# A six-stage decoder kernel on one core: the gated-linear-attention loop in another order, its value and gate products in three f16 passes, and the scales of the last weights moved

## The chip, the core and the metric

The kernel runs on one NeuronCore of a Trainium2 chip. Its engines have queues of their own and meet only through semaphores: TensorE (PE; its weight loads are shown as PEld), VectorE (DVE), ScalarE (ACT), GpSimd (POOL) and SyncE (SP), which here only issues DMAs. The metric is the device time of one execution in microseconds, lower is better; a kernel's time is the median of its runs.

## The reference, cut to what matters

The reference is a decoder of two layers over 2 x 512 tokens of width 128, with six residual stages: gated linear attention (GLA), cross attention to 77 context rows, a layer with a small attention and eight experts, an attention with 16 heads and a position bias, a bidirectional attention with the context, and a feed-forward layer with quantised weights. The change lies in the first stage and in the preparation for the last:

```python
def step(S, inp):
    qt, kt, vt, gt = inp
    S = jnp.exp(gt)[:, None] * S + kt[:, None] * vt[None, :]
    return (S, qt @ S)
...
v = (x @ Wv).reshape(b, t, H, HV).transpose(0, 2, 1, 3)
o = jax.vmap(jax.vmap(_gla_scan))(q, k, v, g)
o = o * jax.lax.rsqrt(jnp.mean(o * o, axis=-1, keepdims=True) + EPS) * rms_w
o = o.reshape(b, t, DV) * jax.nn.silu(x @ Wg)
```

and, for the last stage, `scale = 127.0 / amax` per column of `W_in` and per row of `W_out`, with the weights rounded on that scale.

## The kernel before, in words

Tokens stand in eight tiles of 128 (`NT`), four to each of the two sequences (`TG`). The kernel is one program in which each engine's instructions are written out in order, with explicit semaphores (`sm[...]`): an engine waits with `wait_ge` and everything behind the wait in its queue waits too. No planner sets the order.

The GLA scan is done in chunks of 64 tokens (`CH`), two to a tile. Around the loop of lines 1115 to 1127 TensorE does five things for a tile `i`, each a function:

- `gla_kv(i)` (line 1059): the keys of each chunk times its values, two matmuls of 256 columns on the two 64-row halves of the array (64*128). DVE's `gla_state` turns them into the running state `ST`.
- `gla_a(i)` (L1042): keys times queries, two matmuls of 256 columns on the two 64-column halves (128*64). DVE's `gla_mask` writes the masked product to `AM`.
- the first half of `gla_o(i)` (L1070): `AM` times the values, four matmuls of 64 columns, each with weights of its own, on the whole array (128*128).
- the second half of `gla_o(i)` (L1077): the queries times the state, on 64-column halves again. Its end (`o_mm`) lets ACT square the sum (`take_o`, L704), after which DVE multiplies it with the gate (`gate_out`, L1746), which frees the bank (`ob_ready`).
- `gla_vg(i + 2)` (L1084): the values and the gate of the tile two ahead, one f32 matmul of 512 columns on the whole array. ACT copies the values out (L687) and applies the SiLU (L690).

An f32 matmul shows as two instructions in the trace. The order in an iteration is kv(i), a(i+1), o(i) in its two halves, vg(i+2), so the shape of the array tile changes five times. On DVE the order of an iteration `i` is `gla_state(i)`, `gla_mask(i + 1)`, `gate_out(i - 1)`, and in iterations 1 to 3 one part of `weight_scales` (L1769 to L1779), which takes the maxima of the last stage's weights `wC` and the scales from them; its last part raises `ws_ready`. In iteration 6 `head_norm(0)` (L1754) follows, and TensorE's `gla_t(0)`, in iteration 7, waits for it.

The waits that matter in the loop are these:

```python
# gla_o(i), ahead of its first half
pe.wait_ge(sm["kpt_ready"], min(i, 1) + 1)
pe.wait_ge(sm["am_ready"], i + 1)
if i >= 2:
    pe.wait_ge(sm["ob_ready"], i - 1)
```

that is, the masked product of tile i and `gate_out(i - 2)`. In iteration 0, `keys_t(1)` (four transposes, after DVE's `keys_out(1)`, L1696) stands behind `gla_o(0)`.

POOL sets constants, scales the output weights in `wA` (L415), waits for DVE's queries (`qs_ready`), spreads them over `QX` (L424, L430) and expands the keys of the context (L437). Later, during the cross attention, it splits the first experts' weights (L479, L481), then waits for `ws_ready` and rounds the last weights in four instructions (`quantise_weights`, L461 to L468), then copies the attention values of the first sequence (L494, `at_pool`), for which TensorE's `attended_t(0)` waits. DVE's queue at the end of the cross attention is: `norm_stats(2, 0, X)`, `ctx_norm(6)`, `norm_rows(3, 0, X, Z)`, `norm_rows(2, 0, X, Y)`, `ctx_norm(7)`, the residual; some way on come the products of queries and keys `PR` (L1864).

`norm_rows` is line 1648, `take_yt` (the copy of the transposed normed rows to `YT`, semaphore `ln_yt`) line 640, `keep_busy` (matmuls of ones whose result nobody reads) line 972, and every transpose line 967.

Of the kernel before, what the change touches and what calls it, by code (L numbers as in the profile page):

```python
# [4 lines left out]


# [1 line left out]

# [1 line left out]

# [4 lines left out]
F16 = mybir.dt.float16  # L15
# [5 lines left out]
NT = 8  # L21
# [86 lines left out]
def build(nc, x, cols, rows, wa, gk2, wb, wc, ctx_rows, cst, spread, of_head, onehot, rel_bias, w1, w2, twqkv, two, out):  # L108
    bias_dram = nc.dram_tensor("bias_rows", [TH, P, NREL], F32, kind="Internal").ap()
    stack = ExitStack()  # L110
    with stack:
# [78 lines left out]
        with ExitStack() as held:  # L190
            def gla(name, shape):
                return held.enter_context(nc.sbuf_tensor(name, shape, F32))

            H1 = gla("H1", [LR, TOK])
            U = gla("U", [P, TOK])
            LA = gla("LA", [P, TOK])
            reset = gla("reset", [P, TOK])
            G = gla("G", [P, TOK])
            GC = gla("GC", [P, TOK])
            dG = gla("dG", [P, NC])  # L200
            E0 = gla("E0", [P, TOK])
# [12 lines left out]
            KVM = gla("KVM", [P, DV])  # L214
            ST = gla("ST", [P, 4, DV])
            OB = gla("OB", [P, NT, DV])
            SQ = QX[:, 0:NT // 2, :, :].rearrange("p t h c -> p (t h c)").rearrange("p (t d) -> p t d", d=DV)
            SS = gla("SS", [P, NT * GH])
            SL = gla("SL", [P, NT * GH])
            SR = gla("SR", [P, NT * GH])  # L220
            OT = V[:, :, :].rearrange("p t d -> p (t d)").rearrange("p (n c) -> p n c", n=2)
# [38 lines left out]
        with ExitStack() as held:  # L260
# [53 lines left out]

        names = """ld_x ld_cs ld_a ld_b ld_c ld_d bias_dma dve_c act_c qx_ready qx_pool konst_ready
            ln_var ln_rstd ln_y ln_tp ln_yt x_done
            qk_mm gk_mm h1_ready rc_ready u_ready l_ready g_ready e_ready kp_ready qs_ready kp_tp kpt_ready vg_mm vg_ready
            a_mm am_ready kv_mm st_ready o_mm ob_ready sq_ready sr_ready og_ready ot_mm ot_ready go_mm
            cx_mm cx_copied cx_parts vx_ready vs_mm vb_ready qt_mm qt_hi qt_ready xb_ready s_mm px_sub px_ready pt_mm pt_ready xo_mm ct_ready ws_ready co_mm
            qkv_mm qkv_ready sc_ready se_ready at_pool at_ready att_mm att_ready pr_mm h2_ready rt_mm lg_ready le_ready xh_ready  # L320
            ym_hi ym_ready w1_split w2_split w1_ld0 w1_ld1 w2_ld0 w2_ld1 hid_mm gel_ready hid_hi hid_lo eo_mm acc_ready
            bias_mm bias_ready tw0 tw1 tw_split ld_wo ld_band strip_ready ow_ready ctw_ready
            pj_mm pj_hi pj_ready ts_mm ttr_ready ttr_turn exp_ready rps_ready rpp_ready raw_ready tt_mm pta_ready ptb_ready tpv_mm ctt_ready wo_mm to_ready
            rh_ready rj_mm rj_ready bs_mm m_ready as_sub as_exp as_ready ast_mm ast_ready hq_mm ast_low hq_ready mt_mm mrow_ready mb_mm nm_ready eb_ready hb_mm w0_ready f_mm
            wq_ready wqt_mm win_ready ax_ready ax_mm am_one ab_mm nr_ready yr_ready zs_ready zr_ready zt_mm zt_ready hm_mm ht_ready hq2_ready fo_mm st_out""".split()
        sm = {n: sem(n) for n in names}
# [69 lines left out]
        def _(pool):  # L396
# [566 lines left out]
        def _(pe):  # L963
# [24 lines left out]
            def wA_(name, n):  # L988
                return wA[:, WA[name]:WA[name] + n]
# [69 lines left out]
                    mm(bank[2 + r][:, 0:DV], KPT[CH * r:CH * r + CH, i, :], V[CH * r:CH * r + CH, i, :],  # L1059
                       start=True, stop=True).then_inc(sm["kv_mm"], 1)  # L1060

            def gla_o(i):
                pe.wait_ge(sm["kpt_ready"], min(i, 1) + 1)
                pe.wait_ge(sm["am_ready"], i + 1)
                if i >= 2:
                    pe.wait_ge(sm["ob_ready"], i - 1)
                o = bank[4 + i % 2]
                firsts = 2 * i % CB == 0
                for h in range(GH):
                    ins = mm(o[:, GV * h:GV * h + GV], AM[:, i % 2, h, :], V[:, i, GV * h:GV * h + GV],  # L1070
                             start=(h == 0), stop=False, skip_group_check=True)
                for r in range(2):
                    c = 2 * i + r
                    if c % CB == 0:
                        continue
                    pe.wait_ge(sm["st_ready"], c // CB * (CB - 1) + c % CB)
                    ins = mm(o[CH * r:CH * r + CH, 0:DV], QP[:, CH * c:CH * c + CH], ST[:, c % 4, :],  # L1077
                             start=False, stop=True, skip_group_check=True)
                ins.then_inc(sm["o_mm"], 1)

            def gla_vg(t):

                pe.wait_ge(sm["vg_ready"], gate_at(t - 2))
                mm(bank[6 + t % 2][:, :], YT[:, P * t:P * t + P], wA_("vg", 2 * DV), start=True, stop=True).then_inc(sm["vg_mm"], 1)  # L1084

            def gla_t(g):

# [26 lines left out]
            keep_busy(5, 2)  # L1114
            for i in range(NT):
                gla_kv(i)
                if i + 1 < NT:
                    gla_a(i + 1)
                if i == NT - 1:
                    gla_t(0)  # L1120
                    spread_values()
                    gla_out(0)
                gla_o(i)
                if i == 0:
                    keys_t(1)
                if i + 2 < NT:
                    gla_vg(i + 2)

            def queries(g):

# [494 lines left out]
        def _(dve):  # L1625
# [157 lines left out]
            for i in range(NT):  # L1783
                gla_state(i)
                if i + 1 < NT:
                    gla_mask(i + 1)
                if i >= 1:
                    gate_out(i - 1)
                if 1 <= i < TG:
                    weight_scales(i - 1)  # L1790
                if i == NT - 2:
                    head_norm(0)
            gla_residual(0)
# [36 lines left out]
            for i in range(NT):  # L1830
                if i == NT - 1:

                    dve.wait_ge(sm["x_done"], 3)
                    norm_stats(2, 0, X)
                if i == TG + 1:
                    dve.wait_ge(sm["co_mm"], TG)
                    dve.wait_ge(sm["xb_ready"], 1)
                    residual(0, XB, 7, 1)
                if i == NT - 1:
                    ctx_norm(NT - 2)  # L1840
                if i + 1 < NT:
                    subtract_max(i + 1)
                if i == 0:
                    norm_rows(1, 1, X, Y)
                if i == 1:
                    query_low(1)
# [137 lines left out]
            def t5_step(i, n, s, last):  # L1984
# [9 lines left out]
                if on(s, 1, last):  # L1994
                    if r1 % ROWS == 0:
                        dve.wait_ge(sm["strip_ready"], (i * 2 + r1 // ROWS + 1) * 6)
                    if s >= 5:
                        dve.wait_ge(sm["tt_mm"], (n - 4) * 2)
                    dve.wait_ge(sm["ts_mm"], n * 2)
                    dve.sem_inc(sm["ttr_turn"], 1)  # L2000
# [353 lines left out]
```

## Time and profile before

| | us |
|---|---|
| median of 3 runs | 471.5 |
| the runs | 470.9, 471.5, 475.05 |
| span of the profiled execution, first to last instruction | 473.3 |
| TensorE busy in it | 437.0 (92%) |
| VectorE busy | 361.5 (76%) |
| ScalarE busy | 287.7 (61%) |
| GpSimd busy | 212.3 (45%) |

The profiled execution has no other time of its own beside its span; the span lies between the runs and 1.8 above their median. In the rows of the timeline the columns are: start in us from the span's start, length in us, engine, line, operation, what is written and read, shapes, how many instructions the row merges, and in brackets the idle time of that engine just before, with what released it. Matmul lengths overlap each other, so the distance from start to start is what a stage takes.

### The profile page before, as it was taken

To read this page: it belongs to the slowest core of one execution; us is meant where nothing else is said; L and a number is where in the kernel's file an instruction comes from. 1 tells how busy PE (TensorE), PEld (TensorE's weight loads), DVE (VectorE), ACT (ScalarE), POOL (GpSimd) and SP (SyncE) were. 2 spreads that over 40 slices of the span, in tenths; PEclk is the share of its full clock that TensorE was granted. 3 is DMA by queue.
4 is the path that set the end of the run, shared out by engine and by line. 5 is a ranking of instruction groups with operands and counts; after the bars stand their busy time and mean duration, and the time that the engine had idled before them with its cause. 6 is when DMAs were issued, how large, how long until landed. Compare 5 with 4: busy or idle time off the path is not lost.

```text
span 473.3 us, 13124 instructions
## 1 busy us (share of the span) xinstructions
PE 437.0 (92%) x4544; PEld 311.4 (66%) x4544; DVE 361.5 (76%) x984; ACT 287.7 (61%) x684; POOL 212.3 (45%) x548
## 2 busy tenths in 40 slices
PE   8999887997789998699999999999999997998887
PEld 6555565776667777367666666666666665887756
DVE  3897659775779989777778787777787867557786
ACT  3753436874368874577777777777777776423450
POOL 5160011650123557037766668576666676440200
PEclk9999799998989999899999999999999999999989
DMA  7499936400001131000000000000000000000001
GB/s 218 76 98 100 98 39 201 156 4 1 0 2 35 44 91 35 1 1 18 3 18 3 1 17 14 3 0 0 0 0 0 2 1 2 1 3 1 1 0 46
DMA packets 15622, 15.81 MB, mean 33 GB/s; under 512 B 1348, under 2 KB 12859, under 8 KB 15579
## 3 DMA queue, kind: packets, MB, share of 16 engines
q1 hardware_dynamic: 15579, 15.24, 15.9%
q8 instruction: 26, 0.43, 0.4%
q14 instruction: 17, 0.14, 0.1%
HBM read 10.52 MB, written 4.72 MB: 32 GB/s over the span
## 4 chain that ended last, share of the span: by engine, by line
PE 74%; DVE 18%; ACT 4%; issue 3%; DMA 1%; POOL 0%; SPq 0%; DVEq 0%; ACTq 0%; POOLq 0%
PE bank L967 16%; PE bank L1484 12%; PE bank L1436 10%; PE bank L1359 5%; PE bank L1280 3%; PE bank L1267 3%; PE bank L1477 3%; PE bank L1355 3%; PE bank L1168 2%; PE bank L1374 2%; DVE Y L1648 1%; PE bank L972 1%; PE bank L1070 1%; PE bank L1084 1%; PE bank L1618 1%
## 5 line engine op out<-in xcount | busy, mean ns | idle before, releaser
L877 ACT ACTIVATE SN<-SN,nmx 128x512 f32<-128x512 f32 x128 | 92.7, 725 | 9.7 <-DVE nmx L2016 7.6
L967 PE MATMUL bank<-cs,SN 128*128 128x128 f32 x512 | 67.7, 275 | 3.3 <-DVE Z L2009 1.6
L967 PEld LDWEIGHTS bank<-cs,SN 128*128 128x128 f32 x512 | 57.7, 142 | 18.4 <-issue 12.5
L1436 PE MATMUL bank<-TK,TQ 64*128 64x512 f16 x384 | 52.6, 380 | 1.4 <-DVE TK L1979 1.4
L552 POOL TENSOR_TENSOR CTW<-YT 128x128 f32<-128x128 f32 x64 | 29.6, 462 | 50.9 <-DVE YT L2014 50.6
L2001 DVE CUSTOM_DVE_ANT_0 SN<-bank,strip 128x512 f32<-128x512 f32 x64 | 43.3, 677 | 1.2 <-PE bank L1436 0.6
L2016 DVE CUSTOM_DVE_ANT_0 SN<-bank,strip 128x512 f32<-128x512 f32 x64 | 43.6, 681 | 0.0
L2009 DVE COPY PTO<-bank 128x512 f32<-128x512 f32 x32 | 22.1, 691 | 21.0 <-PE bank L1484 19.2
L972 PE MATMUL bank<-ones 128*128 128x128 f32 x230 | 34.8, 310 | 1.0 <-POOL konst L400 1.0
L972 PEld LDWEIGHTS bank<-ones 128*128 128x128 f32 x230 | 32.5, 222 | 3.9 <-issue 2.5
L2009 DVE COPY Z<-bank 128x512 f32<-128x512 f32 x32 | 22.1, 691 | 16.8 <-PE bank L1484 14.3
L888 ACT COPY PTO<-bank 128x512 f32<-128x512 f32 x32 | 18.7, 586 | 26.1 <-PE bank L1484 26.1
L1484 PE MATMUL bank<-PTO,TV 128*64 128x128 f32 x512 | 33.4, 273 | 0.0
L1484 PE MATMUL bank<-Z,TV 128*64 128x128 f32 x512 | 33.4, 273 | 0.0
L888 ACT COPY Z<-bank 128x512 f32<-128x512 f32 x32 | 18.7, 585 | 22.5 <-PE bank L1484 22.3
L556 POOL TENSOR_TENSOR CTX<-CTW,CTX 128x128 f32 (+1 forms) x64 | 27.4, 428 | 10.0 <-POOL CTX L554 8.7
L554 POOL TENSOR_TENSOR CTX<-CTW,ones 128x128 f32 (+1 forms) x64 | 25.7, 401 | 10.5 <-POOL CTW L552 9.3
L1359 PE MATMUL bank<-YP,WP 128*128 128x512 f16 x96 | 27.2, 398 | 0.6 <-DVE YP L1968 0.6
L2014 DVE COPY YT<-bank 128x256 f32<-128x256 f32 x64 | 26.6, 415 | 1.3 <-PE bank L1484 1.3
L1484 PEld LDWEIGHTS bank<-Z,TV 128*64 128x64 f32 x512 | 27.3, 137 | 0.0
L1484 PEld LDWEIGHTS bank<-PTO,TV 128*64 128x64 f32 x512 | 27.3, 137 | 0.0
L1908 DVE TENSOR_TENSOR HID<-PT,HID 128x512 f16<-128x512 f32 x32 | 24.8, 816 | 2.6 <-ACT HID L809 2.3
(326 smaller groups left out, 965.6 us busy)
## 6 DMA issues: line engine op xcount, KB each, us to landing
bias_rows<-biasr SPq DMA_DIRECT2D x1, 4096.0 KB, 45.2
band<-bias_rows SPq DMA_DIRECT2D x1, 3072.0 KB, 11.2
wqkv<-in_twqkv SPq DMA_DIRECT2D x8, 192.0 KB, 2.7
w1s<-in_w SPq DMA_DIRECT2D x8, 128.0 KB, 2.1
w2s<-in_w SPq DMA_DIRECT2D x8, 128.0 KB, 2.1
wB<-in_wb SPq DMA_DIRECT2D x1, 753.0 KB, 6.0
wA<-in_wa SPq DMA_DIRECT2D x1, 520.0 KB, 4.7
X<-in_x SPq DMA_DIRECT2D x2, 256.0 KB, 3.3
```

Of the source, the lines that this page charges most:

```text
L552: gp.tensor_tensor(CTW[:, :], raw[:, 0:P], raw[:, P:2 * P], ALU.mult).then_inc(sm["ctw_ready"], 1)
L556: gp.tensor_tensor(dst[:, 1, :], CTW[:, :], dst[:, 0, :], ALU.subtract).then_inc(sm["ctt_ready"], 1)
L877: sc.activation(p, p, ACT.Exp, bias=nmx[:, r % RING, h:h + 1], scale=-1.0, accum_out=psm[:, r % RING, h:h + 1]).then_inc(sm["exp_ready"], 1)
L888: sc.copy(probs_t(r, 0), bank[4][:, :]).then_inc(sm["pta_ready"], 1)
L967: return nc.tensor.transpose(out_, in_, ident[0:n, 0:n])
L972: mm(bank[b][:, 2 * P:3 * P], ones[:, :], ones[:, :], start=True, stop=True)
L1359: ins = mm(o[:, :], WP[u][:, w_part, w:w + P], YP[:, x_part, S * g:S * g + S], start=(k == 0), stop=(k == 2))
L1436: ins = mm(bank[2 * (s % 2) + h][:, :], TQ[u][r, q_part, S * b + P * qt:S * b + P * qt + P], TK[u][r, k_part, S * b:S * b + S], start=(k = ...
L1484: ins = mm(bank[6][d, 0:P], TV[u][:, TG * b + kt, d], probs_t(r, h)[:, P * kt:P * kt + P], start=(kt == 0), stop=(kt == TG - 1))
L2001: vv.tensor_tensor_reduce(out=SN[:, r1 % RING, 0, :], in0=bank[2 * (r1 % 2)][:, :], in1=strip[u1][:, 0, c1:c1 + S], scale=-1.0, scalar=3.0 ...
L2009: vv.tensor_copy(probs_t(r, 1), bank[5][:, :]).then_inc(sm["ptb_ready"], 1)
L2016: vv.tensor_tensor_reduce(out=SN[:, r1 % RING, 1, :], in0=bank[2 * (r1 % 2) + 1][:, :], in1=strip[u1][:, 1, c1:c1 + S], scale=-1.0, scalar ...
```

## The change

1. The loop's order on TensorE becomes kv(i), first half of o(i) (now `gla_inside`), vg(i+2), a(i+1), second half of o(i) (now `gla_before`). In iteration 0 `keys_t(1)` stands behind `gla_inside(0)`; in iteration 7 `gla_t(0)`, `spread_values` and `gla_out(0)` stand ahead of `gla_inside(7)` as they stood ahead of `gla_o(7)`. The waits of the halves are the same. DVE's and ACT's orders in the loop stay, but for 3.
2. `gla_vg` of tiles 2 to 7 multiplies f16 halves in three passes (high x high, high x low, low x high). POOL makes them before it scales `wA`: two instructions on the 512 columns of the weights, two on the 256 of tiles 2 and 3, two on the 512 of tiles 4 to 7. Tiles 0 and 1 stay f32.
3. The three parts of `weight_scales` leave the loop and stand in the cross attention's last iteration, behind `ctx_norm(6)` and ahead of `norm_rows(3, 0, X, Z)`.
4. The increments of a semaphore that nobody waits for (`ttr_turn`) go to the new semaphore `vg_split`.

```diff
+            def split_gla(dst, w, n):
+                gp.tensor_tensor(dst[:, 0, :], w, ones[:, 0:1].to_broadcast([P, n]), ALU.mult).then_inc(sm["vg_split"], 1)
+                at = next(parts)
+                pool.wait_ge(sm["vg_split"], at)
+                gp.tensor_tensor(dst[:, 1, :], w, dst[:, 0, :], ALU.subtract).then_inc(sm["vg_split"], 1)
+
+            parts = itertools.count(1, 2)
+            pool.wait_ge(sm["ld_a"], 48)
+            split_gla(WVG, wA[:, WA["vg"]:WA["vg"] + 2 * DV], 2 * DV)
+            for g, (a, b) in enumerate(((2 * P, S), (S, TOK))):
+                pool.wait_ge(sm["ln_yt"], g + 1)
+                split_gla(YG[:, :, a - 2 * P:b - 2 * P], YT[:, a:b], b - a)
...
                 pe.wait_ge(sm["vg_ready"], gate_at(t - 2))
-                mm(bank[6 + t % 2][:, :], YT[:, P * t:P * t + P], wA_("vg", 2 * DV), start=True, stop=True).then_inc(sm["vg_mm"], 1)
+                pe.wait_ge(sm["vg_split"], 4 if t < TG else 6)
+                for k, (x_part, w_part) in enumerate(PRODUCTS):
+                    ins = mm(bank[6 + t % 2][:, :], YG[:, x_part, P * (t - 2):P * (t - 1)], WVG[:, w_part, :], start=(k == 0), stop=(k == 2))
+                ins.then_inc(sm["vg_mm"], 1)
...
             for i in range(NT):
                 gla_kv(i)
-                if i + 1 < NT:
-                    gla_a(i + 1)
                 if i == NT - 1:
                     gla_t(0)
                     spread_values()
                     gla_out(0)
-                gla_o(i)
+                gla_inside(i)
                 if i == 0:
                     keys_t(1)
                 if i + 2 < NT:
                     gla_vg(i + 2)
+                if i + 1 < NT:
+                    gla_a(i + 1)
+                gla_before(i)
...
                 if i >= 1:
                     gate_out(i - 1)
-                if 1 <= i < TG:
-                    weight_scales(i - 1)
...
                 if i == NT - 1:
                     ctx_norm(NT - 2)
+                    for part in range(3):
+                        weight_scales(part)
```

## Rows read from the trace of the kernel before

**Rows 1.** The page: the chain that ended last, shares by engine.

```profile
PE 74%; DVE 18%; ACT 4%; issue 3%; DMA 1%; POOL 0%; SPq 0%; DVEq 0%; ACTq 0%; POOLq 0%
```

**Rows 2.** Windows: stretch, length, busy time of each engine, granted clock, DMA.

```profile
26.00:53.00 27.00, 27.00 (x152) 14.01 (x152) 22.76 (x52) 12.97 (x68) 5.96 (x11) 1.00 0.91 99
...
54.50:55.00 0.50, 0.15 (x1) 0.15 (x2) 0.50 (x2) 0.00 (x0) 0.00 (x0) 0.50 0.91 98
...
61.50:62.00 0.50, 0.50 (x7) 0.50 (x6) 0.00 (x0) 0.00 (x0) 0.00 (x0) 1.00 0.91 98
```

**Rows 3.** Timeline of TensorE, matmuls of one iteration of the GLA loop.

```profile
38.01 0.70 PE L1059 MATMUL bank<-V,KPT 64*128 64x256 f32 x2
38.63 0.65 PE L1042 MATMUL bank<-QX,KC 128*64 128x256 f32 x4
39.22 1.10 PE L1070 MATMUL bank<-V,AM 128*128 128x64 f32 x8
40.25 0.65 PE L1077 MATMUL bank<-ST,QP 128*64 128x256 f32 x4
40.83 1.12 PE L1084 MATMUL bank<-wA,YT 128*128 128x512 f32 x2
```

**Rows 4.** Timeline of TensorE's weight loads, the next iteration's first.

```profile
41.89 0.30 PEld L1059 LDWEIGHTS bank<-V,KPT 64*128 64x128 f32 x4 [0.76 <-issue]
```

**Rows 5.** Timeline of VectorE, one iteration without a part of the scales.

```profile
46.50 0.42 DVE L1737 TENSOR_TENSOR KVM<-bank,cs 128x256 f32<-128x256 f32 x1 [1.13 <-PE bank L1059]
...
48.46 0.86 DVE L1719 TENSOR_TENSOR AM<-bank,cs 64x256 f32<-64x256 f32 x2
...
49.35 0.42 DVE L1746 TENSOR_TENSOR OB<-bank,SG 128x256 f32<-128x256 f32 x1
...
50.39 0.42 DVE L1737 TENSOR_TENSOR KVM<-bank,cs 128x256 f32<-128x256 f32 x1 [0.62 <-PE bank L1059]
```

**Rows 6.** Timeline of TensorE, f16 passes of 512 columns in the experts.

```profile
141.95 2.12 PE L1267 MATMUL bank<-YM,w1p 128*128 128x512 f16 x9 [0.59 <-ACT PT L814]
```

**Rows 7.** Timeline of VectorE, keys of the second sequence, and the end of the loop.

```profile
26.60 1.10 DVE L1696 TENSOR_TENSOR KP<-KC,ED 128x512 f32<-128x512 f32 x1
...
53.58 1.22 DVE L1754 TENSOR_TENSOR OB<-OB,SR 128x1024 f32<-128x1024 f32 x1
```

**Rows 8.** Timeline of TensorE, eight transposes behind the loop and eight later.

```profile
54.85 1.97 PE L967 MATMUL bank<-cs,OB 128*128 128x128 f32 x8 [1.67 <-DVE OB L1754]
...
69.26 1.09 PE L967 MATMUL bank<-cs,OB 128*128 128x128 f32 x8 [0.59 <-DVE OB L1754]
```

**Rows 9.** Timeline of POOL and VectorE, start of the kernel and first iterations.

```profile
11.98 0.61 POOL L415 TENSOR_TENSOR wA<-wA,rmsc 128x256 f32<-128x256 f32 x1 [5.30 <-DMA rmsc<-in_rows]
...
15.79 0.69 DVE L1685 SCALAR_TENSOR_TENSOR U<-U,LA 128x512 f32<-128x512 f32 x1 [0.75 <-ACT LA L660]
...
28.11 1.22 POOL L437 TENSOR_TENSOR KX<-KB,inside 128x616 f16<-128x616 f32 x1
...
28.64 0.97 DVE L1738 SCALAR_TENSOR_TENSOR ST<-ST,E,KVM 128x256 f32<-128x256 f32 x1
...
35.46 0.48 DVE L1738 SCALAR_TENSOR_TENSOR ST<-ST,E,KVM 128x256 f32<-128x256 f32 x1
```

**Rows 10.** Timeline of VectorE, the scales in the loop, and the cross attention's end.

```profile
34.29 0.68 DVE L1773 TENSOR_REDUCE amw<-wC 128x4 f32<-128x512 f32 x1
...
41.31 0.20 DVE L1777 RECIPROCAL scw<-amw 128x8 f32<-128x8 f32 x1
...
111.04 1.12 DVE L1648 TENSOR_SCALAR Y<-X,mv,rstd 128x128 f32<-128x128 f32 x4 [2.92 <-ACT rstd L633]
...
119.72 1.70 DVE L1864 TENSOR_TENSOR PR<-QKV 128x128 f32<-128x128 f32 x8 [1.65 <-ACT QKV L775]
```

**Rows 11.** Timeline of POOL, rounding of the last weights, attention values.

```profile
91.51 1.90 POOL L461 TENSOR_TENSOR WQ<-wC,scw 128x1024 f32<-128x1024 f32 x1
...
116.42 1.03 POOL L494 COPY AT<-QKV 128x128 f32<-128x128 f32 x4 [15.30 <-ACT QKV L775]
```

More of the change, by code:

```diff
@@ L7 @@
 from contextlib import ExitStack
+import itertools
 import numpy as np
@@ L217, in build @@
             SQ = QX[:, 0:NT // 2, :, :].rearrange("p t h c -> p (t h c)").rearrange("p (t d) -> p t d", d=DV)
+            YG = held.enter_context(nc.sbuf_tensor("YG", [P, 2, TOK - 2 * P], F16))
+            WVG = held.enter_context(nc.sbuf_tensor("WVG", [P, 2, 2 * DV], F16))
             SS = gla("SS", [P, NT * GH])
@@ L316, in build @@
             ln_var ln_rstd ln_y ln_tp ln_yt x_done
-            qk_mm gk_mm h1_ready rc_ready u_ready l_ready g_ready e_ready kp_ready qs_ready kp_tp kpt_ready vg_mm vg_ready
+            qk_mm gk_mm h1_ready rc_ready u_ready l_ready g_ready e_ready kp_ready qs_ready kp_tp kpt_ready vg_mm vg_split vg_ready
             a_mm am_ready kv_mm st_ready o_mm ob_ready sq_ready sr_ready og_ready ot_mm ot_ready go_mm
@@ L322, in build @@
             bias_mm bias_ready tw0 tw1 tw_split ld_wo ld_band strip_ready ow_ready ctw_ready
-            pj_mm pj_hi pj_ready ts_mm ttr_ready ttr_turn exp_ready rps_ready rpp_ready raw_ready tt_mm pta_ready ptb_ready tpv_mm ctt_ready wo_mm to_ready
+            pj_mm pj_hi pj_ready ts_mm ttr_ready exp_ready rps_ready rpp_ready raw_ready tt_mm pta_ready ptb_ready tpv_mm ctt_ready wo_mm to_ready
             rh_ready rj_mm rj_ready bs_mm m_ready as_sub as_exp as_ready ast_mm ast_ready hq_mm ast_low hq_ready mt_mm mrow_ready mb_mm nm_ready eb_ready hb_mm w0_ready f_mm
@@ L1060, in gla_kv, with gla_inside @@
                        start=True, stop=True).then_inc(sm["kv_mm"], 1)
-            def gla_o(i):
+            def gla_inside(i):
                 pe.wait_ge(sm["kpt_ready"], min(i, 1) + 1)
@@ L1066, in gla_o, with gla_before @@
                     pe.wait_ge(sm["ob_ready"], i - 1)
-                o = bank[4 + i % 2]
-                firsts = 2 * i % CB == 0
                 for h in range(GH):
-                    ins = mm(o[:, GV * h:GV * h + GV], AM[:, i % 2, h, :], V[:, i, GV * h:GV * h + GV],
-                             start=(h == 0), stop=False, skip_group_check=True)
+                    mm(bank[4 + i % 2][:, GV * h:GV * h + GV], AM[:, i % 2, h, :], V[:, i, GV * h:GV * h + GV],
+                       start=(h == 0), stop=False, skip_group_check=True)
+            def gla_before(i):
                 for r in range(2):
@@ L1076, in gla_o @@
                     pe.wait_ge(sm["st_ready"], c // CB * (CB - 1) + c % CB)
-                    ins = mm(o[CH * r:CH * r + CH, 0:DV], QP[:, CH * c:CH * c + CH], ST[:, c % 4, :],
+                    ins = mm(bank[4 + i % 2][CH * r:CH * r + CH, 0:DV], QP[:, CH * c:CH * c + CH], ST[:, c % 4, :],
                              start=False, stop=True, skip_group_check=True)
@@ L1999, in t5_step @@
                     dve.wait_ge(sm["ts_mm"], n * 2)
-                    dve.sem_inc(sm["ttr_turn"], 1)
+                    dve.sem_inc(sm["vg_split"], 1)
                     vv.tensor_tensor_reduce(out=SN[:, r1 % RING, 0, :], in0=bank[2 * (r1 % 2)][:, :], in1=strip[u1][:, 0, c1:c1 + S], scale=-1.0,
```

## The prediction

> **What bounds the kernel now.** I read the chain of waits first: TensorE carries 74% of it and VectorE 18% [rows 1]. The change touches four places, so I then took windows: through the GLA loop, 26 to 53 us, TensorE is busy 27.00 of 27.00 us at full clock [rows 2]. There TensorE sets the pace and nobody keeps it waiting. The timeline gives its lap. From start to start kv takes 0.62, a 0.59, the first half of o 1.03, its second half 0.58 and vg 1.06 [rows 3], and the next kv starts at 41.89 [rows 4]: 3.88 us. VectorE works 3.27 of that in an iteration without the scales (46.50 to 50.39 less 0.62 idle): state 1.96, mask 0.89 (48.46 to 49.35), gate_out 0.42 [rows 5]. So there is 0.6 us between the two engines, and a faster TensorE soon meets VectorE. That is the question here, and it is one of order more than of sums.
>
> **TensorE's own lap after.** Five changes of the array tile become three: inside and vg share the whole array, a and before share the 64-column halves. What a change costs can't be read from one row. Below: a has two passes of 256 columns one behind the other in 0.59, vg two of 512 in 1.06 [rows 3], so 2 x 0.59 - 1.06 = 0.12 is what a stage has beside its columns. Above: the 0.76 that the weight load of kv stands after the loads of vg [rows 4], most of which is vg streaming. I take 0.15, near the lower end, since the upper one holds columns. The f16 product: nine passes of 512 columns take 2.12, 0.236 each with what fills them [rows 6]; three take 0.71, against 1.06 - 0.12 = 0.94 for the f32 columns. That saves 0.23; if the passes hold all of a stage's other cost, 1.06 - 0.71 = 0.35; if f32 and f16 cost alike in this place, nothing. I take 0.25. Then kv is 0.62, inside with vg 1.03 + 1.06 - 0.15 - 0.25 = 1.69, a with before 0.59 + 0.58 - 0.15 = 1.02: 3.33 us, 0.55 less than now.
>
> **The ring that takes its place.** In the old order a(i+1) comes right behind kv(i), so mask(i+1) has until the next iteration's first half of o, more than a lap of TensorE's work. Now a(i) is followed by before(i-1) and kv(i) alone, and then inside(i) waits for mask(i) and for gate_out(i-2). VectorE does gate_out(i-2) directly behind mask(i), since its order is unchanged. Behind the waiting inside(i) stand vg(i+2), a(i+1) and before(i) in TensorE's queue, and mask(i+1) waits for that a. This closes a ring: a's end to mask 0.05, mask 0.89, gate_out 0.42 [rows 5], to TensorE 0.05 (head_norm ends at 54.80, the transposes start at 54.85 [rows 7, 8]), inside with vg 1.69, a until its end 0.65 [rows 3]. Sum 3.75 us. It is longer than TensorE's 3.33 and VectorE's 3.27, so it sets the lap: 0.13 less than before, not 0.55, and TensorE stands some 0.4 us in each lap in front of inside.
>
> **From the first lap to the last.** gate_out enters at i = 2, so the first laps run at TensorE's pace. VectorE's keys of the second sequence end at 27.70 [rows 7] as now, the work ahead of them being the same. keys_t(1) starts 27.75 and takes half of the eight later transposes' 1.09 [rows 8], 0.55; vg(2) 0.81 (1.06 - 0.25) to 29.11; a(1) and before(0) to 30.13; kv(1) to 30.75; mask(1) is ready at 30.67 (a(1) ends 29.76, 0.05, 0.86). Inside(1) and vg(3) to 32.44, a(2) ends 33.09. Four laps of 3.75 later a(6) ends at 48.09, gate_out(4) 1.36 later at 49.45. kv(6) is done by then (49.16). VectorE's state(6) takes 1.96 to 51.45 with a handover, a(7) is done earlier (51.18), mask(7) 0.89, gate_out(5) 0.42: head_norm(0) starts at 52.8. It starts at 53.58 now [rows 7]. The loop gives **0.8 us**. With 0.12 and 0.23 in place of 0.15 and 0.25 a lap is 3.80 and the gain 0.5; with nothing from f16 the ring is 4.00 and the stage ends 0.7 later than now; with the whole 0.76 for a change the ring falls under VectorE's 3.27 and TensorE's pace, about 3.3, and some 3.3 us are gained. After head_norm the queue is as before.
>
> **POOL's split, at the start.** Six instructions: four of 512 columns, two of 256. The nearest rows are 1.22 for 616 columns [rows 9] and 1.90 for 1024 [rows 11]; 1.0 to 1.1 for 512, half for 256: 5.4 us, and the scaling of wA behind them 0.61 [rows 9]. POOL is free from 6.68 (5.30 idle before 11.98) and the loads it waits for are issued ahead of those that let it go at 11.98 [rows 9], so it ends between 12.7 and 18.0. Its next work waits for queries at 22, and vg(2) comes at 28.3: hidden. The cost can only be a meeting on VectorE: ST takes 0.97 beside POOL's 1.22, 0.48 without [rows 9], and U, with two SBUF inputs, is on the path at 15.79. Between 0 and 1.5 (three such operations, up to 18); the middle of POOL's two ends is 15.4, so I take 0.1.
>
> **The scales, later.** In the loop they are 0.68 twice and four small ones of about 0.2 [rows 10], 2.2 us, and TensorE waited for none of it: nothing gained by taking them out. (Left in the new ring they would push mask past a's end.) At the new place VectorE has 2.92 idle before Y at 111.04 [rows 10], and 2.2 fit; without that cover they would cost 2.2. But POOL's rounding now starts at about 109.1 instead of 91.51. It took until 101.12 (116.42 - 15.30) [rows 11], 9.6 us, so it ends at 118.7, and the copies of 1.03 [rows 11] at 119.8, where they ended at 117.45. PR starts at 119.72 [rows 10]: they just miss it. Cost 0; if POOL is a microsecond later, PR beside it loses about half of its 1.70, 0.85. Nothing is gained where the rounding left. No DMA is moved, and no queue of SP.
>
> **Sum.** -0.8 + 0.1 + 0 = -0.7: the span goes from 473.3 to 472.6. The runs shown have a median of 471.5, 1.8 below that span, so against them 470.8.
>
> **Rivals.** (1) TensorE stays the bound. For it: no idle in 27 us [rows 2]. Against it: the ring above. Six laps at 0.55 less: -3.3, 468.2. (2) The clock. TensorE stands 1.67 before the transposes at 54.85 and the granted clock is 0.50 there and 1.00 again at 61.5 [rows 2, 8]; eight transposes take 1.97 instead of 1.09. The idle stretch will be about as long (kv(7) ends at 52.3, head_norm at 54.0), so nothing says that the fall goes; but if it comes elsewhere in the work, 6.4 us at 1.09/1.97 are worth 2.8 us: 468.0, and a new fall somewhere costs as much: 473.6. (3) On the other side: POOL's split runs past 15.8. It decides from a start after 9.6, and then U, the scan behind it and the second U meet it, 0.5 each, on a path without slack: -0.8 + 1.5 = +0.7, 472.2. The Trainium skill (SBUF — State Buffer, "SBUF: two separate sides") has a rule that speaks for this one: VectorE with two SBUF inputs and a reading GpSimd operation share an exclusive lock, and the later one stands until the other is done. By that rule U would wait up to a whole split operation, 1.1 for the first of the three; the trace shows a stretch of 0.49 inside 0.69 of overlap, which agrees in kind [rows 9]. (4) The rounding meets PR: 471.7. (5) The change doesn't do what it says: f16 passes with their three weight loads cost what f32 did; ring 4.00, 472.2.
>
> **Chances.** Ring as forecast 0.52 (own range 469.8 to 471.4), TensorE bound 0.13, clock 0.12 (most of it for the better), split at the start 0.10, rounding 0.07, no gain from f16 0.06. A measurement of this kernel tells 1%, 4.7 us, from no change: faster by more needs (1) and (2) together, 0.06; slower by more needs a run like the 475.05 and a rival besides, 0.04; the rest 0.90. The range reaches from just under (1) and (2), 467.4, to (3) and (5) with part of a new clock fall, 473.2.
>
> **What would show it.** The ring: TensorE idle in front of the first half of o, released by VectorE's OB, about 0.4 us in each iteration from i = 2; lap 3.75; head_norm at 52.8. The changes: inside to vg and a to before without a gap. The split: POOL done by 16, U still 0.69. The scales: VectorE idle before Y at 111 shrinks from 2.92 to about 0.7, POOL's rounding to 118.7, PR still 1.70. I am wrong if TensorE has no idle in the loop or if the lap is under 3.5 or over 3.9.

## The result and the profile after

| | before | after |
|---|---|---|
| median, us (18 runs each, in turn) | 473.86 | 478.91 |
| lowest to highest | 470.87 to 476.1 | 474.57 to 482.39 |
| span of the profiled execution | 473.3 | 477.4 |
| TensorE busy | 437.0 | 434.4 |
| VectorE busy | 361.5 | 366.5 |
| GpSimd busy | 212.3 | 218.1 |

The changed kernel is slower: ratio 1.0111, 95% interval 1.0085 to 1.0138, or 5.05 us between the medians. Three of the changed kernel's runs (481.97 to 482.39) are over 1.5% above its fastest; without them the difference is 4.8. The forecast was 0.7 less, within 1%; the result lies outside its range.

Read in three places, the difference is this. The milestones are starts of instructions in the two profiled executions.

| milestone | before | after | lag |
|---|---|---|---|
| `U`, the scan of the gates begins | 12.85 | 16.07 | +3.22 |
| `head_norm(0)`, end of the GLA loop | 53.58 | 56.32 | +2.74 |
| last norm rows ahead of the cross attention (`Y`) | 78.46 | 81.33 | +2.87 |
| norm rows `Z` of the first sequence, cross attention's end | 107.00 | 111.45 | +4.45 |
| norm rows `Y` behind them | 111.04 | 114.93 | +3.89 |
| norm rows `Z` of the second sequence | 115.86 | 120.26 | +4.40 |
| `PR` | 119.72 | 124.67 | +4.95 |

So the start loses 3.2, the loop gives back 0.48, and the cross attention's end, with the scales and the rounding, loses another 2.1 (4.95 - 2.87).

**The start.** The timeline of the kernel after, start of the kernel, all engines:

```profile
7.07 3.97 DVE L1671 TENSOR_SCALAR Y<-X,mv,rstd 128x128 f32<-128x128 f32 x8
...
8.69 1.04 POOL L418 TENSOR_TENSOR WVG<-wA,ones 128x512 f16<-128x512 f32 x1 [2.01 <-DMA colp<-in_cols]
...
9.80 1.15 POOL L421 TENSOR_TENSOR WVG<-wA,WVG 128x512 f16<-128x512 f32 x1
...
11.09 1.11 PE L984 MATMUL bank<-cs,Y 128*128 128x128 f32 x4 [2.17 <-DVE Y L1671]
...
12.14 2.77 PE L1019 MATMUL bank<-YT,wA 128*16 128x512 f32 x4
...
16.07 1.53 DVE L1696 TENSOR_SCALAR U<-bank,colp 128x512 f32<-128x512 f32 x2 [5.04 <-PE bank L1022]
```

The same places in the kernel before, VectorE and TensorE:

```profile
7.04 2.10 DVE L1648 TENSOR_SCALAR Y<-X,mv,rstd 128x128 f32<-128x128 f32 x8
...
9.79 1.89 PE L1002 MATMUL bank<-YT,wA 128*16 128x512 f32 x4
...
12.85 1.53 DVE L1673 TENSOR_SCALAR U<-bank,colp 128x512 f32<-128x512 f32 x2 [3.70 <-PE bank L1005]
```

The eight normed rows `Y` take 3.97 us, where the same line of before took 2.10. Narrow windows of VectorE show two of the eight singly:

```profile
8.58 1.23 DVE L1671 TENSOR_SCALAR Y<-X,mv,rstd 128x128 f32<-128x128 f32 x1
...
9.73 1.31 DVE L1671 TENSOR_SCALAR Y<-X,mv,rstd 128x128 f32<-128x128 f32 x1
```

The first ends at 9.81, POOL's first product at 9.73; the second ends at 11.04, POOL's second at 10.95. Each row that began beside a product of POOL ended 0.08 or 0.09 after it: these products did not slow the rows, each held one row for as long as it ran. The Trainium skill describes that (SBUF — State Buffer, "SBUF: two separate sides"): a VectorE operation that uses both ports and a GpSimd operation lock each other out, and the one that starts first keeps the ports for its whole length. The Trainium skill (VectorE: DVE Perf Modes, "Mode 2×_2P") counts a `tensor_scalar` from SBUF to SBUF among the operations with both ports, though it has one tensor input. The two rows agree with the lock and its length. They don't show that the first to start wins: by the profile's starts both rows began before the product that held them (8.58 and 8.69, 9.73 and 9.80). Further on two kinds of POOL's instructions, L480 and memsets, don't keep to the length either; there the measurement decides.

TensorE waited 2.17 us for these rows, and the windows show what followed (columns as in [rows 2]):

```profile
10.50:11.00 0.50, 0.00 (x0) 0.00 (x0) 0.50 (x1) 0.00 (x0) 0.50 (x2) 0.53 0.54 103
11.00:13.50 2.50, 2.41 (x6) 0.99 (x7) 0.04 (x1) 0.58 (x1) 1.79 (x3) 0.50 0.47 88
14.00:16.00 2.00, 2.00 (x6) 0.66 (x4) 0.00 (x0) 1.15 (x2) 1.72 (x2) 1.00 0.31 125
```

The granted clock is at 0.50 while the transposes and L1019 run, and at full again at 14: the four transposes take 1.11 instead of 0.66 and L1019 2.77 instead of 1.89. So 1.9 us of held rows became 3.2 us at `U`.

**The loop.** The window that answers to the first of [rows 2]:

```profile
26.00:53.00 27.00, 24.18 (x159) 14.08 (x158) 21.37 (x45) 14.84 (x63) 7.84 (x14) 1.00 0.91 99
```

The timeline of one lap, of TensorE, its weight loads and VectorE, which answers to [rows 3], [rows 4] and [rows 5]:

```profile
39.50 0.65 PE L1059 MATMUL bank<-QX,KC 128*64 128x256 f32 x4
...
40.51 0.70 PE L1076 MATMUL bank<-V,KPT 64*128 64x256 f32 x2
41.72 1.08 PE L1086 MATMUL bank<-V,AM 128*128 128x64 f32 x8 [0.51 <-DVE OB L1769]
42.63 0.81 PE L1105 MATMUL bank<-WVG,YG 128*128 128x512 f16 x3
43.37 0.65 PE L1059 MATMUL bank<-QX,KC 128*64 128x256 f32 x4
...
41.69 0.97 PEld L1086 LDWEIGHTS bank<-V,AM 128*128 128x128 f32 x8 [0.88 <-issue]
...
40.25 0.86 DVE L1742 TENSOR_TENSOR AM<-bank,cs 64x256 f32<-64x256 f32 x2 [0.72 <-PE bank L1059]
41.14 0.42 DVE L1769 TENSOR_TENSOR OB<-bank,SG 128x256 f32<-128x256 f32 x1
```

TensorE, busy all 27 us before, now stands 0.5 us in each lap, released by VectorE's `OB`. From one a to the next the lap is 43.37 - 39.50 = 3.87 us (3.88 before).

**The cross attention's end.** VectorE's and POOL's timelines of the kernel after, which answer to [rows 10] and [rows 11]:

```profile
109.29 1.40 DVE L1796 TENSOR_REDUCE amw<-wC 128x4 f32<-128x512 f32 x2
...
111.45 3.55 DVE L1671 TENSOR_SCALAR Z<-X,mv,rstd 128x128 f32<-128x128 f32 x4
114.93 1.63 DVE L1671 TENSOR_SCALAR Y<-X,mv,rstd 128x128 f32<-128x128 f32 x4
...
120.26 1.84 DVE L1671 TENSOR_SCALAR Z<-X,mv,rstd 128x128 f32<-128x128 f32 x4 [0.61 <-ACT rstd L647]
...
124.67 1.71 DVE L1887 TENSOR_TENSOR PR<-QKV 128x128 f32<-128x128 f32 x8 [1.54 <-ACT QKV L792]
...
111.62 1.92 POOL L478 TENSOR_TENSOR WQ<-wC,scw 128x1024 f32<-128x1024 f32 x1 [16.23 <-DVE inw L1802]
113.63 2.78 POOL L480 TENSOR_SCALAR WQ<-WQ 128x1024 f32<-128x1024 f32 x1
...
120.22 1.04 POOL L485 TENSOR_TENSOR WQ<-WQ,inw 128x512 f32<-128x512 f32 x1
```

and two of VectorE's rows in the kernel before:

```profile
107.00 1.11 DVE L1648 TENSOR_SCALAR Z<-X,mv,rstd 128x128 f32<-128x128 f32 x4
...
115.86 1.18 DVE L1648 TENSOR_SCALAR Z<-X,mv,rstd 128x128 f32<-128x128 f32 x4 [0.60 <-ACT rstd L630]
```

The scales begin with L1796, and the rounding starts directly behind them, where the norm rows stand too. Four rows `Z` take 3.55; the same four took 1.11 in before. Narrow windows show the second one, held until 0.09 after L478's end at 113.54, and the third:

```profile
111.71 1.92 DVE L1671 TENSOR_SCALAR Z<-X,mv,rstd 128x128 f32<-128x128 f32 x1
...
113.55 1.20 DVE L1671 TENSOR_SCALAR Z<-X,mv,rstd 128x128 f32<-128x128 f32 x1
```

The third ends at 114.75, beside L480, which runs until 116.41. So not every instruction of POOL holds a row for its whole length: L480 let rows through in its middle. `Y` behind them takes 1.63 against 1.12 [rows 10], the next `Z`, beside L485, 1.84 against 1.18. `PR`, for which the forecast had watched, is not touched: 1.71 against 1.70 [rows 10].

From these the milestones can be worked out. The scales delay `Z` by 1.58 (4.45 - 2.87), and `Z` is 2.44 longer. VectorE's 2.92 of idle time ahead of `Y` [rows 10] take in all of the first, but not both: 1.58 + 2.44 - 2.92 = 1.1, and `Y` is 1.02 late (3.89 - 2.87). `Y` itself adds its 0.51, and the second sequence's `Z` is 1.53 late; of its own 0.66, 0.55 arrive at `PR`. Together 2.1.

### The profile page after: what moved, and what is told of

Read it like the earlier page. It is cut to its first block, busy times and chain, and to the rows that moved or that the text cites. A ratio compares the mean times of both kernels' runs of the same rounds, so it can differ in the third digit from the quotient of the medians.

```text
span 477.4 us, 13149 instructions
## 1 busy us (share of the span) xinstructions
PE 434.4 (91%) x4550; PEld 310.8 (65%) x4550; DVE 366.5 (77%) x984; ACT 288.4 (60%) x684; POOL 218.1 (46%) x554
## 4 chain that ended last, share of the span: by engine, by line
PE 71%; DVE 21%; issue 3%; ACT 3%; DMA 1%; POOL 0%; DVEq 0%; SPq 0%; POOLq 0%
PE bank L984 16%; PE bank L1507 12%; PE bank L1459 10%; PE bank L1382 5%; PE bank L1290 4%; PE bank L1303 3%; PE bank L1500 3%; PE bank L1378 3%; PE bank L1191 2%; PE bank L1397 2%; DVE Y L1671 2%; PE bank L1086 1%; DVE Z L1671 1%; DVE stats L1660 1%; PE bank L1641 1%
## 5 line engine op out<-in xcount | busy, mean ns | idle before, releaser
L989 PE MATMUL bank<-ones 128*128 128x128 f32 x230 | 33.4, 301 | 1.0 <-POOL konst L404 1.0
L989 PEld LDWEIGHTS bank<-ones 128*128 128x128 f32 x230 | 31.2, 214 | 3.9 <-issue 2.5
L1459 PEld LDWEIGHTS bank<-TK,TQ 64*128 64x128 f16 x384 | 13.5, 94 | 20.0 <-issue 9.9
```

The source lines that it names most:

```text
L989: mm(bank[b][:, 2 * P:3 * P], ones[:, :], ones[:, :], start=True, stop=True)
L1459: ins = mm(bank[2 * (s % 2) + h][:, :], TQ[u][r, q_part, S * b + P * qt:S * b + P * qt + P], TK[u][r, k_part, S * b:S * b + S], start=(k = ...
```

## The experiments

The theory: POOL's operations, wherever they stand beside VectorE's norm rows, hold those rows; that is the start's 3.2 us and the 2.1 at the scales, and the loop itself gains 0.5. The rivals: the loop's order or its f16 products cost the time, or the additional work of VectorE at the scales does. Runs 1, 2, 4 and 8 have their runs of the kernel before in common, and so have runs 3, 5, 6 and 7 (medians 473.74 and 474.91). Runs of one kernel scatter by up to 8 us (474.57 to 482.39 for the kernel after), and their mean granted clock goes with it: runs of before at 0.993 took 470.9 to 471.0, at 0.975 476.6 to 477.8. So what an edit does locally is read from the profiles, and the medians are only a check on its sign. Where the two differ, runs of an equal mean granted clock are compared.

**1. The kernel after, with the split waiting for the norm rows of both sequences.**

```diff
             pool.wait_ge(sm["ld_a"], 48)
+            pool.wait_ge(sm["ln_y"], 2)
             split_gla(WVG, wA[:, WA["vg"]:WA["vg"] + 2 * DV], 2 * DV)
```

> The changed kernel, with POOL's split held back until VectorE's first norm rows (Y) are done. Theory (lock): POOL's split kept VectorE's TENSOR_SCALAR rows out for 1.9 us at 9 us, TensorE stood, its clock fell, and U came 3.2 us late. So Y's eight rows take 2.1 again instead of 3.97, U starts at about 12.9 instead of 16.07, head_norm(0) at about 53.1 instead of 56.32, the median falls by 3.2 to some 475.7. Rival (the loop): the ring of 3.87 us a lap and its idle TensorE lose the time; then U comes early but the median stays within 1 us of 478.9. Rival (clock falls only, by luck of where they come): no steady difference, 478.9.

Measured 473.87 us, ratio to before 1.002 (0.9976 to 1.0065). Its timeline at the start, VectorE and POOL:

```profile
7.07 2.11 DVE L1672 TENSOR_SCALAR Y<-X,mv,rstd 128x128 f32<-128x128 f32 x8
...
9.34 1.04 POOL L418 TENSOR_TENSOR WVG<-wA,ones 128x512 f16<-128x512 f32 x1 [2.65 <-DVE Y L1672]
```

The rows are back at 2.11, `U` starts at 12.89 and `head_norm(0)` at 53.14, 0.44 ahead of before. Splitting 0.65 later costs nothing. The start's loss is settled: it is the meeting of the split with `Y`. The four rows `Z` still take 3.56. Against the median of the kernel after it gains 5.0, more than the local 3.2, but those two were not run in turn. Nor does the median show the 2.1 that the scales still cost here; at a mean granted clock of 0.978 it shows, with 476.70 to 476.75 against 474.95 to 476.42 of before.

**2. The kernel after, with the scales taken right behind the GLA loop.**

```diff
+            for part in range(3):
+                weight_scales(part)
             gla_residual(0)
...
                     ctx_norm(NT - 2)
-                    for part in range(3):
-                        weight_scales(part)
```

> The changed kernel, with the weights' scales ahead of the first GLA residual, where VectorE is idle for 6 us, instead of in the cross attention's end. Theory (lock): POOL's rounding then runs at 95 to 105 us beside VectorE operations that read PSUM; the Z rows take 1.11 instead of 3.55, the Y rows 1.11 instead of 1.63, and the next Z rows 1.2 instead of 1.84; the median falls by about 2.1 to 476.8. Rival (the scales themselves are too long for their gap): the same fall, but then the scales alone would have filled VectorE's idle time and the rows would not have been stretched. Rival (loop): no change, 478.9.

Measured 475.02, ratio 1.0059 (1.0002 to 1.0116); one of the ten runs took 825.76, and without it the median is 473.94. `Z` takes 1.12 again, `Y` 1.11, the next `Z` 1.18. The start is still hit, but by one product only, since the loads that POOL waits for (the last, by the profile, is `colp`) let it start at 8.86 here instead of 8.69. VectorE's and POOL's rows of this run:

```profile
7.14 2.91 DVE L1671 TENSOR_SCALAR Y<-X,mv,rstd 128x128 f32<-128x128 f32 x8
...
8.86 1.11 POOL L418 TENSOR_TENSOR WVG<-wA,ones 128x512 f16<-128x512 f32 x1 [2.17 <-DMA colp<-in_cols]
...
105.84 1.12 DVE L1671 TENSOR_SCALAR Z<-X,mv,rstd 128x128 f32<-128x128 f32 x4
```

The rows lose 0.80, but `U` starts at 15.41, 2.56 late: TensorE stood 1.11 and the granted clock was at 0.50 from 10.9 to 14, so L1019 took 3.55 instead of 1.89.

**3. The kernel after with both.** The edits of 1 and 2 together.

> The changed kernel with both mends: POOL's split behind the first norm rows, the scales where VectorE is idle ahead of the first GLA residual. Theory (lock in two places): U at 12.9, head_norm(0) at 53.1, every norm row at its old length (four in 1.1 to 1.2), POOL's rounding at 93 to 103; the median 0.3 to 0.6 under that of before, 473.3, ratio 0.998 to 1.000. Rival (loop): if the loop's ring loses the time, it stays 3 to 5 over before.

Measured 472.19, ratio 0.9954 (0.9917 to 0.9991). `Y` 2.11, `U` 12.89, `head_norm(0)` 53.12, `Z` 1.12, the rounding from 92.33 on. With both meetings out, the loss is gone. That it is 2.7 us ahead of before, where the loop gives 0.46, isn't explained by the profile: this kernel's profiled execution took 476.05, with falls of the clock at 55, 113 and 137 us. The table behind run 7 settles most of it: the means of runs with an equal mean clock are 1.2 apart at 0.989, 0.1 at 0.978 and 0.8 at 0.975.

**4. The kernel before, with the scales alone moved.** The change's part 3 and nothing else:

```diff
                     gate_out(i - 1)
-                if 1 <= i < TG:
-                    weight_scales(i - 1)
...
                     ctx_norm(NT - 2)
+                    for part in range(3):
+                        weight_scales(part)
```

> The kernel before with only the scales moved to the cross attention's end. Theory (lock): Z rows 3.5 instead of 1.11, Y rows about 1.6, the next Z rows about 1.8, the whole 1.5 to 2.2 slower than before, 475.4 to 476.0. Rival (loop): the loop is untouched, the time is that of before, 473.9; if anything 0.3 less, for VectorE's shorter queue in three iterations.

Measured 476.48, ratio 1.0061 (1.0019 to 1.0103): 2.7 us slower. VectorE's and POOL's rows at the cross attention's end:

```profile
107.20 3.55 DVE L1648 TENSOR_SCALAR Z<-X,mv,rstd 128x128 f32<-128x128 f32 x4
...
107.38 1.92 POOL L461 TENSOR_TENSOR WQ<-wC,scw 128x1024 f32<-128x1024 f32 x1 [16.65 <-DVE inw L1779]
```

Counted from the last norm rows ahead of the cross attention (77.09 here, 78.46 in before), `Z` starts 30.11 later instead of 28.54, `PR` (at 120.43) 43.34 later instead of 41.26: 1.57 and 2.08 more, the kernel after's 1.58 and 2.1 without anything of its start or loop. In run 2, where scales and rounding stand elsewhere, `PR` comes 40.47 later. So part 3 of the change costs 2.1 by itself against before, and 2.9 against run 2, whose granted clock did not fall in this stretch; before's was at 0.50 from 112.5 to 115.5 and this run's from 110 to 116.5, so the share of the falls isn't separated. Had the rows kept their 1.11, the scales' 1.57 would have been within the 2.92 of idle time; it is the held rows that go beyond it. That is worked out: no run has the scales in this place and the rounding in another.

**5. The mended kernel with DVE's two instructions of a lap swapped.** On top of 3:

```diff
                 gla_state(i)
-                if i + 1 < NT:
-                    gla_mask(i + 1)
                 if i >= 1:
                     gate_out(i - 1)
+                if i + 1 < NT:
+                    gla_mask(i + 1)
```

> As the one with both mends, and VectorE does gate_out(i-1) ahead of mask(i+1). Theory (ring through mask and gate_out): the 3.87 us lap loses gate_out's 0.36 to 0.42; the ring is then 0.10 + 0.89 + 0.13 + 1.69 + 0.65 = 3.46, VectorE's own queue about 3.4; lap 3.4 to 3.5, head_norm(0) at about 51.0 instead of 53.1, the median some 2 under that with both mends, ratio to before about 0.995. Rival (TensorE or the array changes set the 3.87): the lap stays 3.87 and head_norm at 53.1.

Measured 470.02, ratio 0.9912 (0.988 to 0.9945), the fastest of all and faster than both kernels. TensorE's rows:

```profile
41.05 1.09 PE L1087 MATMUL bank<-V,AM 128*128 128x64 f32 x8
...
44.38 1.09 PE L1087 MATMUL bank<-V,AM 128*128 128x64 f32 x8
```

No idle time stands behind these rows, and the lap is 3.33, the forecast's own figure for TensorE alone. `head_norm(0)` starts at 50.98. The ring was the bound, and `gate_out` behind the mask closed it. The lap is under the 3.4 to 3.5 that was expected: that sum took 0.10 from a's end to the mask, and here a ends at 43.37 and the mask starts at 43.42.

**6. The mended kernel with the f32 product of before**, so the new order alone. The halves are still made and nobody reads them.

```diff
-                pe.wait_ge(sm["vg_split"], 4 if t < TG else 6)
-                for k, (x_part, w_part) in enumerate(PRODUCTS):
...
+                mm(bank[6 + t % 2][:, :], YT[:, P * t:P * t + P], wA_("vg", 2 * DV), start=True, stop=True).then_inc(sm["vg_mm"], 1)
```

> As the one with both mends, but the values and gates stay one f32 product (POOL's halves are made and not used): the new order alone. Theory (ring): vg is in the ring, so the f32 product lengthens the lap from 3.87 by what f16 saves, 0.2 to 0.25: lap 4.1, over the old 3.88, head_norm at 54.2, later than before. Rival (array changes): two changes fewer show as a lap under 3.88.

Measured 472.7, ratio 0.9981 (0.9939 to 1.0023). TensorE's rows:

```profile
39.22 1.08 PE L1087 MATMUL bank<-V,AM 128*128 128x64 f32 x8 [0.51 <-DVE OB L1767]
43.36 1.08 PE L1087 MATMUL bank<-V,AM 128*128 128x64 f32 x8 [0.50 <-DVE OB L1767]
```

The lap is 4.14, longer than the old order's 3.88, though TensorE changes its array tile less often. `head_norm(0)` starts at 54.62, 1.04 later than in before.

**7. The mended kernel in the old order**, so the f16 products alone.

```diff
                 gla_kv(i)
+                if i + 1 < NT:
+                    gla_a(i + 1)
...
                 gla_inside(i)
+                gla_before(i)
...
-                if i + 1 < NT:
-                    gla_a(i + 1)
-                gla_before(i)
```

> As the one with both mends, but the loop in the old order: the f16 products alone. Theory: TensorE sets the lap and the mask has its old lead, so the lap falls by what f16 saves, 0.2 to 0.25, to 3.65, and head_norm comes at about 52.3, 0.8 ahead of the new order. Rival (the new order is what gains): the lap stays at 3.8 to 3.9.

Measured 472.01, ratio 0.9945 (0.99 to 0.9989). TensorE's rows:

```profile
38.42 1.10 PE L1087 MATMUL bank<-V,AM 128*128 128x64 f32 x8
42.01 1.10 PE L1087 MATMUL bank<-V,AM 128*128 128x64 f32 x8
```

The lap is 3.59, 0.29 under before and without idle time; `head_norm(0)` starts at 51.88. With DVE's order as it is, the f16 products alone do more in the loop than products and new order together.

The medians of runs 3, 5, 6 and 7 all lie 2.2 us or more under that of before, run 6 too, whose loop is longer. Runs of an equal mean granted clock (before's are those that these four have in common) follow the profiles instead:

| kernel | `head_norm(0)` against before | runs at a mean clock of 0.989, us | at 0.975 |
|---|---|---|---|
| before | | 471.62 to 472.32 | 476.65 to 477.83 |
| run 3 | -0.46 | 470.33 to 470.94 | 475.88 to 476.11 |
| run 5 | -2.60 | 468.72, 468.91 | 473.74 |
| run 6 | +1.04 | 472.02, 472.23 | 477.44 |
| run 7 | -1.70 | 469.57, 469.60 | none |

The rest of the medians' lead is that more of these runs had a high clock. Whether the edits bring that about or chance does isn't shown.

**8. The kernel before, with POOL's split alone.** Old order, f32 products, scales in the loop; POOL makes the halves and nobody reads them.

```diff
+            pool.wait_ge(sm["ld_a"], 48)
+            split_gla(WVG, wA[:, WA["vg"]:WA["vg"] + 2 * DV], 2 * DV)
...
             pool.wait_ge(sm["ld_b"], 64)
```

> The old order, f32 products and the scales in the loop, but POOL makes the f16 halves all the same; nobody uses them. Theory (lock): Y's eight rows take about 4.0, U starts at about 16.1, the loop's lap is 3.88 as before, the median 3.2 over before, 477. Rival (loop): 473.9, since the loop is that of before. Rival (clock): the fall at 10.5 us comes or not by luck; then Y's rows would be 2.1 and U at 12.9 in this run.

Four runs: 475.34, 478.92, 480.19 and 478.3, ratio 1.0106 (1.0013 to 1.0199). The profiled one is the 475.34, and it escaped:

```profile
7.08 2.11 DVE L1668 TENSOR_SCALAR Y<-X,mv,rstd 128x128 f32<-128x128 f32 x8
...
9.24 1.04 POOL L418 TENSOR_TENSOR WVG<-wA,ones 128x512 f16<-128x512 f32 x1 [2.56 <-DMA colp<-in_cols]
```

The loads let POOL start at 9.24 here, and the rows had ended at 9.19. What was expected of the rows was missed by this profile, and it shows why: the landing time decides. POOL's start was 8.69 with two rows held, 8.86 with one, 9.24 with none. The other three runs are 3 to 5 us longer; that their rows were held fits, but isn't seen.

**9 to 11. The disputed cost by itself.** In the kernel before, two POOL operations of 512 columns are put beside the eight rows `Z` ahead of the experts, and write a tile that nobody reads. Each was run once; the rows are what is read.

```diff
+            pool.wait_ge(sm["ld_c"], 16)
+            pool.wait_ge(sm["ln_var"], 10)
+            for k in range(2):
+                gp.tensor_tensor(SCR[:, k, :], wC[:, 0:F1], wC[:, F1:2 * F1], ALU.mult)
             with pool.Fori(0, NE // 2 - 1) as i:
```

In the second kernel the last added line is a copy, in the third a memset:

```diff
+                gp.tensor_copy(SCR[:, k, :], wC[:, 0:F1])
...
+                gp.memset(SCR[:, k, :], 0.0)
```

> The kernel before, and beside VectorE's eight norm rows ahead of the experts (Z, 2.11 us at 132 us) POOL does two products of two SBUF tiles, 512 columns, into a tile that nobody reads. Theory (lock, POOL operations that read two SBUF operands hold the rows): the eight rows take 2.11 plus most of two operations of 1.1 to 1.3, 3.9 to 4.4. Rival (only f16 output or a broadcast operand holds them, or it was the DMA that came in at the start): 2.11.

> The same with two POOL copies of 512 columns (one SBUF operand). The trace of before has copies of 128 columns beside norm rows of 1.18 and 1.10, so either copies don't hold the rows, then 2.11, or the short ones fall between them, then 3.5 to 4.4 here. I expect the latter with 0.6.

> The same with two POOL memsets of 512 columns, which read nothing. If only POOL's reads hold the rows, 2.11; if any POOL operation does, 2.11 plus the two memsets. I expect 2.11 with 0.6.

The eight rows took 2.11 in before:

```profile
132.17 2.11 DVE L1648 TENSOR_SCALAR Z<-H,mv,rstd 128x128 f32<-128x128 f32 x8
```

With the products (this run's time was 478.7):

```profile
132.07 4.07 DVE L1653 TENSOR_SCALAR Z<-H,mv,rstd 128x128 f32<-128x128 f32 x8
...
132.30 2.48 POOL L504 TENSOR_TENSOR SCR<-wC 128x512 f32<-128x512 f32 x2
```

with the copies (474.2), and in narrow windows the first copy and the row that it held:

```profile
130.99 2.73 DVE L1653 TENSOR_SCALAR Z<-H,mv,rstd 128x128 f32<-128x128 f32 x8
...
131.20 1.16 POOL L504 COPY SCR<-wC 128x512 f32<-128x512 f32 x2
...
131.22 0.67 DVE L1653 TENSOR_SCALAR Z<-H,mv,rstd 128x128 f32<-128x128 f32 x1
...
131.20 0.61 POOL L504 COPY SCR<-wC 128x512 f32<-128x512 f32 x1
```

with the memsets (472.71):

```profile
131.04 2.30 DVE L1653 TENSOR_SCALAR Z<-H,mv,rstd 128x128 f32<-128x128 f32 x8
...
131.24 1.19 POOL L504 MEMSET SCR<- 128x512 f32 x2
```

Products cost 1.96 of their 2.48, copies 0.62 of 1.16, memsets 0.19 of 1.19. That products with two inputs hold the rows is shown at a third place of the kernel, with nothing else of the change in it. The copies are between the two answers that were written down: they hold a row each, as was expected with 0.6, but a copy takes 0.61, half of a product, so the cost is under the expected 3.5 to 4.4. Products and copies do the same to a row: it ends 0.08 to 0.09 behind POOL's instruction, and since a row takes 0.26 anyway (eight in 2.11), two instructions cost their time less 0.52, 1.96 for the products and 0.64 for the copies. The memsets don't fit that, though 2.11 was missed too: the row beside a memset ends 0.08 behind it, but the row after it starts as early as ever, and 0.1 is lost for each.

## Why the prediction was wrong

**The step that failed** is the pricing of POOL's work on VectorE. It stood twice in the text. Of the split: "The cost can only be a meeting on VectorE: ST takes 0.97 beside POOL's 1.22 ... and U, with two SBUF inputs, is on the path at 15.79", priced at 0.1. Of the scales, with PR's start in view: "they just miss it. Cost 0". In both I looked only for VectorE operations with two SBUF inputs. Runs 1, 2 and 4 show that the norm rows, with one, are held as well: 1.87 us at the start (3.97 less 2.10), 2.4 at `Z`, 0.5 at `Y`, 0.7 at the next `Z`. Rival 3, the split on the wrong side, named the right mechanism, but at the wrong place and time: it waited for `U` and asked for a split later than 15.8, where the meeting came at 8.7 because the split was *early*. I had written that POOL is free from 6.68 and may be done at 12.7, and did not go through VectorE's timeline of that stretch, where `Y` stands from 7.04 to 9.14. The sign that I had set down for the split, POOL done by 16, came true (15.74), and the loss came all the same.

**What misled.** The rule that I cited from the Trainium skill (SBUF — State Buffer, "SBUF: two separate sides") has two cases, VectorE operations with two SBUF inputs and those that use both ports for one, and I used the first only. The trace before has POOL copies beside such rows with hardly a stretch: the next `Z` took 1.18 and the `Y` behind it 1.10. These are copies of 128 columns, 0.29 long, hardly more than a row takes. A narrow window would have shown the hold even there: one row of that `Z` starts at 116.38 and takes 0.41, until 0.08 behind the first copy.

**A moved step took its follower along.** That VectorE's idle time ahead of `Y` would take in the 2.2 us was right for the scales alone: they delay `Z` by 1.57, within 2.92. I followed the rounding to its new place too, but asked only where it ends, not what stands beside its first instruction, and the held rows use up the idle time and 1.1 us more.

**The loop** came out as forecast in kind: a ring through mask and `gate_out` with TensorE idle in front of `inside`, released by `OB`. TensorE's own terms were right: `inside` with vg 1.68 (from its first load at 41.69 to the next a at 43.37), forecast 1.69; a with before 1.01, forecast 1.02; and 3.33 for all in run 5. The f16 saving, forecast 0.25, is 4.14 - 3.87 = 0.27 in the new order and 0.29 in the old. The 0.15 for a change of the array tile is 0.13: between runs 7 and 5, both without idle time, two changes fewer take 0.26 from the lap (3.59 and 3.33). Rival 5, no gain from f16, is out, and rival 1, TensorE the bound, needs run 5's swap. Mis-sized were the two handovers, each taken as 0.05 from a VectorE-to-TensorE pair [rows 7, 8]: a ends at 40.15 (39.50 + 0.65) and the mask starts at 40.25, 0.10; `gate_out` ends at 41.56 and TensorE's load starts at 41.69, 0.13. The ring is then 0.10 + 0.89 + 0.42 + 0.13 + 1.68 + 0.65 = 3.87 instead of 3.75, and the loop gives 0.48 instead of 0.8. The ends of matmuls are modelled, so the 0.10 is rough; in run 5 the same pair stands 0.05 apart.

**The clock**, rival 2, is a part of the loss: 3.22 at `U` are 1.9 of held rows and some 1.3 of transposes and matmuls at a granted clock of 0.50, in a stretch that ran through in before.

**Slips of the working** decided nothing. By its own figures the copies would end at 119.73, not ahead of `PR` at 119.72. The split, 6.0 us with the scaling, runs past 15.8 from a start after 9.8, not 9.6. And with 0.76 for a change TensorE's own lap would be 2.1; the 3.3 given there is VectorE's.

**The base** was wrong too. The executions of all later profiles are 1.8 us longer than their spans (477.4 and 479.16 after), so the span 473.3 belongs to the run of 475.05. Setting a span below a median mixed the two. Added to the 18-run median of before, the forecast -0.7 would have read 473.2, and the miss would still be 5.7.

The parts add up: 3.2 at the start, less 0.5 in the loop, and 2.1 at the scales are 4.8 in the two profiled executions, against 5.05 between the medians. What the clock falls behind `PR` carry differs between executions and isn't separated.

## What to carry to other kernels

When work is added to or moved on POOL, list every VectorE instruction that can run beside it, from the earliest time at which POOL may start, and price each SBUF-to-SBUF norm row, not only operations with two tensors, at the length of the POOL product beside it. The followers of a moved step have to be listed in the same way. When a new order puts one engine's wait right behind another's result, the order on the second engine has to be changed with it: here, with both meetings out, one swap on VectorE took the lap from 3.87 to 3.33 and the median from 472.19 to 470.02 us, 0.9912 of the kernel before.

## What the runs showed of the hardware

- POOL's products and copies hold a norm row until 0.08 or 0.09 behind their own end. Two of them beside the same eight rows cost 1.96 of 2.48 and 0.62 of 1.16, their time less the 0.26 that each held row takes anyway. Two memsets, which read nothing, cost 0.19 of 1.19, and L480, a `tensor_scalar`, let rows through in its middle. Why these two differ isn't known.
- An operation that reads PSUM was not held: in run 1 the two of `U` take 1.53 from 12.89 on, as in before, with POOL's products at 12.89 and 14.00 beside them.
- A landing time that scatters between executions (POOL's start behind it: 8.69, 8.86, 9.24) decided about 3 us (`U` at 16.07, 15.41, 12.89): whether POOL met the rows was left to chance. Kernel 1's wait removes the chance.
- Changing the array tile less often did not pay by itself: run 6, with three changes, has a longer lap (4.14) than the kernel before with five (3.88), since the order that saves the changes also closes the ring. With the ring open a change is worth 0.13 (run 7 against run 5).
